# Linear-attention layers: V made channel-major like K and Q, sums taken on VectorE, biases in row groups, factors in another form

## What is computed

```python
Q  = elu(x @ Wq[i] + bq[i]) + 1
Kf = elu(x @ Wk[i] + bk[i]) + 1
V  = x @ Wv[i] + bv[i]
KV   = jnp.sum(Kf * V, axis=1)          # over the 256 tokens of a sequence
sumK = jnp.sum(Kf, axis=1)
Z    = 1.0 / (Q * sumK[:, None] + 1e-06)
att  = Q * KV[:, None] * Z
x = _layer_norm(gelu(att @ Wo[i] + bo[i]) + x, ln1_s[i], ln1_b[i])
h = gelu(gelu(x @ W1[i] + b1[i]) @ W2[i] + b2[i])
x = _layer_norm(h + x, ln2_s[i], ln2_b[i])
```

## Time and profile before

| | us |
|---|---|
| median of 3 runs | 4040.78 |
| lowest and highest | 4039.62 and 4046.01 |
| the profiled execution: its span | 4045.9 |
| steady step in the layers (from one second table load of ScalarE to the same of the next step) | 38.9 |

### The profile page before, as it was taken

The page is one execution under the profiler, slowest core; times in us unless marked ns, Lnnn a source line. Parts: engine busy times, 40 slices in busy tenths (PEclk is TensorE's granted clock), DMA queues, the critical chain, the costliest instruction groups (busy, mean ns, idle before and its releaser), DMA issues. The chain is left out here.

```text
span 4045.9 us, 56998 instructions
## 1 busy us (share of the span) xinstructions
PE 3365.3 (83%) x18213; PEld 2365.0 (58%) x18213; DVE 2807.3 (69%) x8434; ACT 2276.1 (56%) x3608; POOL 669.9 (17%) x826
## 2 busy tenths in 40 slices
PE   6998999513339999999999999999999999999664
PEld 5777777413226656666666666565656666666343
DVE  4556555466237787778787778787878777878566
ACT  3444444201127777777676777676767777677420
POOL 0000000104420111112111212111211111211122
PEclk9999999756659999999999999999999999999866
DMA  1000000002310000000000000000000000000000
GB/s 45 0 0 0 0 0 0 14 8 91 41 56 1 1 18 9 4 11 12 7 1 23 7 1 23 7 1 18 9 4 18 9 4 1 1 1 1 6 0 21
DMA packets 31214, 47.81 MB, mean 12 GB/s; under 512 B 3824, under 2 KB 21296, under 8 KB 30960
## 3 DMA queue, kind: packets, MB, share of 16 engines
q1 hardware_dynamic: 25328, 40.52, 3.1%
q0 software_dynamic: 5632, 4.20, 0.8%
HBM read 36.22 MB, written 8.49 MB: 11 GB/s over the span
## 5 line engine op out<-in xcount | busy, mean ns | idle before, releaser
L1432 PEld LDWEIGHTS t_sum_ps<-state,t_feat_k 128*128 128x128 f32 x4096 | 510.2, 192 | 79.2 <-DVE t_kv L1714 54.2
L1443 PE MATMUL t_o_ps<-t_feat_q,t_wo 128*128 128x512 f32 x1024 | 491.7, 603 | 64.0 <-DVE t_feat_q L1702 64.0
L1582 ACT ACTIVATE t_recip<-t_feat_q,t_z_eps,t_sum_k 128x256 f32<-128x256 f32 x1024 | 529.0, 590 | 24.4 <-DVE t_kv_out L1768 14.7
L1432 PE MATMUL t_sum_ps<-state,t_feat_k 128*128 128x129 f32 x4096 | 528.6, 277 | 16.0 <-DVE t_kv L1714 16.0
L1702 DVE SCALAR_TENSOR_TENSOR t_feat_q<-t_feat_q,t_kv_out,t_recip 128x256 f32<-128x256 f32 x1024 | 512.6, 561 | 6.7 <-ACT t_recip L1590 6.7
L1684 DVE SCALAR_TENSOR_TENSOR t_feat_k<-t_exp_k,t_k_ps 128x1024 f32<-128x1024 f32 x256 | 311.1, 1215 | 195.7 <-ACT t_exp_k L1567 195.7
L1567 ACT ACTIVATE t_exp_k<-t_k_ps,t_minus_one 128x1024 f32<-128x1024 f32 x256 | 283.3, 1107 | 274.7 <-PE t_k_ps L1409 274.7
L1572 ACT ACTIVATE t_exp_q<-t_q_ps,t_minus_one 128x1024 f32<-128x1024 f32 x256 | 284.0, 1109 | 186.4 <-PE t_q_ps L1421 186.4
L1418 PE MATMUL t_q_ps<-t_x_hi,t_wqk_hi 128*128 128x512 f32 x512 | 307.2, 600 | 47.6 <-DVE t_feat_q L1690 39.4
L1406 PE MATMUL t_k_ps<-t_wqk_hi,t_x_hi 128*128 128x512 f32 x512 | 289.8, 566 | 42.0 <-POOL t_x_lo L1854 24.0
L1690 DVE SCALAR_TENSOR_TENSOR t_feat_q<-t_exp_q,t_q_ps 128x1024 f32<-128x1024 f32 x256 | 312.6, 1221 | 8.8
(11 more groups left out here) (355 smaller groups left out, 7550.2 us busy)
## 6 DMA issues: line engine op xcount, KB each, us to landing
t_raw_qk<-in_wk SPq DMA_DIRECT2D x8, 512.0 KB
t_raw_qk<-in_wq SPq DMA_DIRECT2D x8, 512.0 KB
t_raw_v<-in_wv SPq DMA_DIRECT2D x8, 512.0 KB, 3.4
t_raw_o<-in_wo SPq DMA_DIRECT2D x8, 512.0 KB, 3.5
t_raw<-in_w SPq DMA_DIRECT2D x16, 256.0 KB, 2.9
x<-in_x SPq DMA_DIRECT2D x4, 512.0 KB, 7.2
tokens_dram<-r_hn SPq DMA_DIRECT2D x8, 256.0 KB, 2.3
e_w_raw<-in_fc_w SPq DMA_DIRECT2D x4, 512.0 KB, 4.2
```

The costliest lines, as they stand in the source:

```text
L1432: last = pe.matmul(sum_ps[:, at * (D + 1):(at + 1) * (D + 1)], feat_k[:, 2 * n + i, chunk * P:(chunk + 1) * P], rows, start=(i == 0), stop ...
L1443: last = pe.matmul(o_ps[:], wo[:, chunk, :], feat_q[:, s, chunk, :], start=(chunk == 0), stop=(chunk == NC - 1), skip_group_check=True)
L1582: last = act.activation(recip[:, q % 2, k * UNIT + n * SEQ:k * UNIT + (n + 1) * SEQ], feat_q[:, s, chunk, cols], ACT.Ln, bias=z_eps[:, 0:1 ...
```

## The change

V is made like K and Q. All three are now channel-major: `three_pass` makes one chunk of 128 channels by 512 tokens in three matmuls, `keys`, `queries` and the new `values` call it. `t_v_ps` is one bank and takes the place of `t_sum_ps`. The bias matmuls of K and Q of a quarter are taken out of `keys` and `queries` and stand together in `biases(t, q)`, ahead of both: four matmuls of three rows each, whose operands start at partitions 0, 32, 64 and 96, each into its own bank. `biases(t, q)` waits for both `k_ready` and `q_ready` of the quarter before it. `values` on VectorE multiplies `t_v_ps` by `t_feat_k` with a sum along the row, two of 256 elements to a chunk; `feature_k` is four instructions of 256 elements, each with the sum of K as its accumulator. `finish_sums` is six operations of 16 elements once a unit. The factor KV Q / (Q sumK + eps) is rewritten as -(1 / (Q sumK / eps + 1) - 1) times KV / sumK, so that `attention` is a `tensor_scalar` of `t_recip` that no longer reads `t_feat_q`. `state` (token-major x), its copies, `swap_v` and the multiplication of Wv go; a third `swap` per layer comes. `stack_entry_phase` loses the turn back and its loop.

```diff
-            def sums(t, n, k):
-                pe.wait_ge(c["sums_drained"], 6 * t + 3 * n + k + 1)
-                        last = pe.matmul(sum_ps[:, at * (D + 1):(at + 1) * (D + 1)], feat_k[:, 2 * n + i, chunk * P:(chunk + 1) * P],
-                                         rows, start=(i == 0), stop=(i == 1))
+            def biases(t, q):
+                pe.wait_ge(c["k_ready"], 4 * t + q + 1)
+                pe.wait_ge(c["q_ready"], 4 * t + q + 1)
+                for kind, out in ((0, k_ps), (1, q_ps)):
+                    for half in range(2):
+                        rows = slice(32 * (2 * kind + half), 32 * (2 * kind + half) + 3)
+                        pe.matmul(out[:, half * UNIT:(half + 1) * UNIT], b3[rows, q, :], ones_b[rows, :],
+                                  start=True, stop=False, skip_group_check=True)
+            def values(t, s, q, half):
+                pe.wait_ge(c["v_drained"], 8 * t + 2 * q + half + 1)
+                three_pass(v_ps[:], 2, 2 * q + half, s, True).then_inc(c["v_filled"], 1)
...
-                        last = dve.scalar_tensor_tensor(a, a, kv_out[:, s, n, chunk:chunk + 1],
-                                                        recip[:, q % 2, k * UNIT + n * SEQ:k * UNIT + (n + 1) * SEQ],
-                                                        ALU.mult, ALU.mult)
+                        last = dve.tensor_scalar(feat_q[:, s, chunk, cols], recip[:, q % 2, k * UNIT + n * SEQ:k * UNIT + (n + 1) * SEQ],
+                                                 -1.0, neg_mean[:, s, n, chunk:chunk + 1], ALU.add, ALU.mult)
...
+                    last = dve.tensor_tensor_reduce(junk[:, n, :], v_ps[:, n * SEQ:(n + 1) * SEQ],
+                                                    feat_k[:, q % 2, k * UNIT + n * SEQ:k * UNIT + (n + 1) * SEQ], 1.0, 0.0,
+                                                    ALU.mult, ALU.add, sum_kv[:, s, n, 2 * q + k:2 * q + k + 1])
```

More of the change, by code:

```diff
@@ L1215, in turn @@
[L1215 to L1225, removed]
+                    t = n * GT + i
@@ L1496, in step @@
                         pe.wait_ge(c["hid_ready"], 4 * (t - 3) + 4)
-                    for i in range(4):
-                        last = pe.transpose(m1[:, i * P:(i + 1) * P], y1[:, i * P:(i + 1) * P], ident)
-                    last.then_inc(c["z1_turned"], 1)
+                    turn(m1, y1, c["z1_turned"])
+                if A:
+                    biases(t, 1)
+                    keys(t, s, 1)
                 if E:
@@ L1526, in step @@
                 if A:
-                    sums(t, 0, 2)
+                    biases(t, 2)
+                    keys(t, s, 2)
+                    queries(t, s, 2)
+                    values(t, s, 2, 0)
+                if C:
+                    pe.wait_ge(c["n1_ready"], 4 * (t - 2) + 5)
+                    turn(m1, y1, c["n1_turned"])
+                if B:
+                    project(t - 1, 1 - s, 1)
+                if A:
+                    values(t, s, 2, 1)
+                    biases(t, 3)
                     keys(t, s, 3)
@@ L1646, in step @@
                         swap(closing, 0)
+                    exp_queries(t, 3)
+                    if closing is not None:
+                        swap(closing, 1)
+                if B:
+                    exp_z(t - 1, 2)
                 if E:
@@ L1793, in step @@
                     dve.tensor_copy(x1_hi[:], x1[:, s, :]).then_inc(c["x1_hi_ready"], 1)
+                if A:
+                    feature_k(t, s, 3)
+                    if closing is not None:
+                        swap_bias(closing)
+                        swap(closing, 0)
+                    values(t, s, 3, 0)
+                    feature_q(t, s, 3)
+                    if closing is not None:
+                        swap(closing, 1)
                 if B:
@@ L1796, in step @@
                 if A:
-                    feature_k(t, 3)
+                    values(t, s, 3, 1)
                     if closing is not None:
-                        swap(closing, 0)
-                    feature_q(t, s, 3)
-                    if closing is not None:
-                        swap(closing, 1)
+                        swap(closing, 2)
             run(dve, step)
```

431 lines of the change are left out of this document (179 added, 252 removed), and 3 rows, old and new, of the table names.

## The result

The changed kernel takes 5028.12 us, median of 4 runs (5024.5 to 5032.9), against 4043.4 for the one before (4 runs, 4039.6 to 4047.7): 1.243 times as long, 95% interval 1.242 to 1.245. Its profiled execution has a span of 5025.1. The prediction said 4888, in 4560 to 5130.

A forecast was written before the change was run, and what follows sets the result against it. The bound was taken to be the serial chain through four quarters plus TensorE's slowed clock, 53.8 us a step against 38.9. From 4045.9, +913 over 61.5 steps, -42 between layers, -24 ahead, -5.1 for the median: 4888 us, range 4560 to 5130.

The forecast's parts named there:

- The bound and the mechanism: From one quarter's queries to the next, exponential, feature_q, attention, projection, biases, keys and queries run without overlap; chance with slower clock 0.62.
- The signs named beforehand: Steady stretch: TensorE under 75% busy, three 3 to 4 us waits a step, clock well under 1.00, step 50 to 56 us.
- The hand-laid chain: One step laid out over four quarters at full clock: 48.7 us, 49.3 with dearer biases and rounding.
- T0 to T1: T0 to T3 are when TensorE has issued a quarter's last query matmul; this first stretch was laid out at 13.55 us.
- The clock: TensorE's slower clock behind idle gaps of 3.0 to 4.0 us: 1.5 us for each of three, 4.5 a step.
- The edges: Between layers about -6 us each, times 7, -42; ahead of the layers -24.
- the count of full steps: Of 68 steps, 61.5 counted as full ones, each 14.85 us longer: +913 us.
- The parts' prices: VectorE's feature_k 4 x 0.345 us, `attention` 1.07 a quarter at 0.27 each; TensorE's biases 0.4 a quarter.
- TensorE's own work: TensorE's work a step falls from 37.1 to 33.6 us, 3.5 less, with biases counted at 1.6.
- The third rival: Engines use each other's slack; a step is TensorE's 33.6 us plus 1.8 of waits, 35.4; 3760 us, chance 0.08.
- The chain without the clock: Rival: the serial chain through the quarters, with TensorE's clock staying up across the gaps; 4612 us, chance 0.16.
- The dear ends together: Rival: serial biases, accumulators at 0.48, clock price 1.65 four times; step 58.9 us, 5205 us in all, chance 0.12.

The follow-up runs named there:

- e1_late: Changed kernel with TensorE's projections of quarters 0, 1 and 2 placed behind the next work that does not wait for the factors; 4326.6 us.
- e2_warm: Changed kernel with dummy matmuls of zero weights (12 + 8, 14 and 14) put where TensorE idled; 4632.6 us.
- e9_joint: e6_order with the four bias matmuls issued together again in quarters 0 and 1; 3927.0 us, 0.971 of the kernel before.
- e5_stt: Changed kernel with `attention` as scalar_tensor_tensor with the mean as broadcast tensor instead of tensor_scalar with a pointer scalar; 5117.6 us.
- e4_onegroup: Changed kernel with all bias operands in partitions 0 to 2, so a quarter's four bias matmuls run one behind the other; 5240.9 us.
- e6_order: Changed kernel's operations in a new order on three engines, with K's and Q's biases waiting apart and projections late; 3938.9 us, 0.974 of the kernel before.
- e7_half: Changed kernel with dummy matmuls in TensorE's gaps, half as many as e2_warm (6 + 4, 7 and 7); 4718.9 us.

## Why the prediction came out as it did

*The bound and the mechanism: right, and shown.* The waits of `t_o_ps` for `t_feat_q` stand where the chain put them, three a step and up to 3.9 long in a steady one; e1_late takes them away and gives 702 us. The signs named beforehand are there, two of them at the edge: TensorE is busy 42.01 of 56.00, which is 75% and not under it, and a step is 56.3 where 50 to 56 was said.

*The hand-laid chain: right.* e2_warm is that chain at the full clock. From the starts of its query matmuls T0 to T1 is 14.0, T1 to T2 13.0, T2 to T3 11.95, T3 to T0 10.5, in all 49.4, where the prediction had 13.55, 13.3, 11.65 and 10.2, with biases and rounding 49.3. So close a sum is in part luck, since single errors cancel in it: the logarithms take 1.62 to the next start and not 2.10, and the second stretch is 0.3 shorter than laid out, but the other three are 0.3 to 0.45 longer. Four transposes ahead of the biases take 0.53 and not 0.43.

*The clock: the term that was mis-sized.* I gave it 1.5 us behind each of three gaps, 4.5 a step. It is 56.3 - 49.4 = 6.9. The row it was taken from had eight matmuls behind the gap and then lighter work; here the stretch goes on: the projection, the values, the biases and the first key matmul all stand in it, 3133.33 to about 3139.4, and each is on the chain. From the start of the projection to the second key matmul the three places take 4.85, 6.09 and 5.99 or 4.96, where e2_warm takes 2.58, 3.28 and 3.28, so a gap costs 1.7 to 2.8 and not 1.5. What lies behind a gap should have been counted for as long as it is on the path, not for as long as one example showed. Over 61.5 steps the missing 2.4 are 148 us. The time was missed by 140, but that the two are so near is luck: the terms below miss by as much again in both directions, and cancel.

*The edges: too small, in the other direction.* The layers' ends give 12.5 us each (14.4 less 1.9), seven times 88, where 42 was predicted. The boundary was longer than I read it: besides the two long stretches in the earlier trace rows there is a step of 41.3 ahead of the one of 45.6, which I had not counted. What became of the rest is not shown; in e9_joint, where the steps hardly wait, an end still costs about 5 (313.7 - 8 x 38.6), so about 3 of the 12.5 may be hidden in steps that wait anyway. The first table load comes 34 us earlier (1161.58 against 1195.92), where 24 was predicted. The turns themselves gave what I said, and I had left out a wait: VectorE's 8.46 for all eight factors at the head of the earlier trace rows is gone, because each turn of the changed kernel waits for its own.

```profile
1122.36 2.10 DVE L1196 TENSOR_SCALAR n_xn<-x,n_moments,n_rstd 128x128 f32<-128x128 f32 x8
1124.73 7.34 DVE L1196 TENSOR_SCALAR n_xn<-x,n_moments,n_rstd 128x128 f32<-128x128 f32 x24 [0.26 <-PE n_turned_x L1206]
```

With the measured terms the sum is 4888 + 61.5 x (56.3 - 53.8) - 46 - 10 = 4986, and 42 are left. Some 34 of them lie in the count of full steps: from the first table load to the last it is 3577 us against 2561, so 1016 over eight layers, which with the 88 of the ends is 63.4 steps of 17.4 and not 61.5. The first layer loses 129 (first load to the ninth: 422.5 against 293.4), although its first steps are short ones that I counted at half. The other 8 are the difference between the profiled executions and the medians.

*The parts' prices: mostly right.* feature_k's four are 0.34 apart with their accumulators (0.345 taken). `attention` is 1.13 long a quarter and 0.26 apart (1.07 and 0.27 taken), and e5_stt shows that the form is what does it. Biases were taken at 0.4 a quarter; measured 0.32 from their start to the next, with the matmul ahead of them 0.09 and the one behind 0.10 longer, so 0.51.

The rule of the Trainium skill that was weighed there ("TensorE: Matmul & The Clock Gate", Part 3, 3.07x for four row tiles) gives 0.31 a quarter, and the trace agrees with 0.32. The drain at a change of tiling mode ("TensorEngine Tiling (Array Packing)", Key Properties) can be no more than those 0.09 and 0.10, and whether it is in them is not shown, since the matmul behind four transposes is as long (0.32 from 3111.26 to the next) without a change of mode.

*TensorE's own work: too low.* The third rival had a step of 35.4 with 33.6 of work. The kernels in the new order come to 38.6 with 2.5 to 2.7 of waits, so about 36 of work. Most of the difference is the biases: in e9_joint they stand in six groups, five of about 0.5 us with the matmuls around them and one of 0.9 in quarter 0, in all 3.4 where 1.6 was counted. The transposes are a part of the rest. The kernel before has about 37.8 by the same count (38.9 with 1.1 of waits), so the change in this order took less than 2 us of work off TensorE and not 3.5. So the faster rival was 3760 on paper and is 3927 in the best order that I ran.

*The rivals.* The chain without the clock (4612) is what e2_warm built: 4633. The dear ends together (5205) come near e4_onegroup, 5241, by the same serial biases and dear clock, and in part by luck, since that case also had accumulators at 0.48. The faster side exists only with the order of e6_order.

## What to carry to other kernels

Before pricing an edit by what it adds to an engine, look for the work that stood between a result and its user, and lay the step out by hand if that work goes: here TensorE's own work fell and the kernel lost a quarter. In this kernel a gap of 3 to 4 us on TensorE cost twice where the work behind it was on the path, once as idle time and once as its slower clock, and the second has to be counted over all of that work. If an edit must take cover away, reorder with it: the same arithmetic was 5028 us in one order and 3927 in another.

## What the runs showed of the hardware

- Matmuls on zero weights hold the granted clock: with them in the gaps it was 1.00 over a step, where it was 0.82 without.
- In the changed kernel every projection behind a wait from 2000 to 3000 us (53, behind 1.95 to 6.1 us) ran slow, and in the step shown the slow matmuls went on for 4 to 6 us, at a granted clock that sank to 0.67 over the stretch. In e7_half 19 of 57 did (behind 1.4 to 4.2 us), and the shorter gaps were not the safer ones: 5 of 5 behind 1.4 to 1.5, none of 14 behind 1.75 to 1.85.
- Four bias matmuls of 3 rows and 512 columns in four row groups take 0.32 us together, and a lone pair as much; in one row group two pairs start 0.83 apart at the lower clock, where the four take 1.81 against 0.55.
- ScalarE's four logarithms of 256 elements take 1.70 with a constant bias and a tile as scale, where they took 2.07 with tiles as both.
